# Graph attention layer and routed experts: first stage with fewer sort steps, skip projection moved, running maxima raised in place

## The chip, the cores and the metric

One core of one Trainium2 chip runs the whole kernel. The metric is the device time of one execution in microseconds (us). The engines are PE (matrix products), DVE (vector), ACT (scalar functions), POOL (GpSimd, which here issues the gathers) and SP (which issues most other DMAs).

## The reference

The input has 6250 nodes with 256 features, and 200000 edges sorted by their destination. First comes a layer norm and one attention layer on the graph, then a small attention that routes nodes to four experts, on 131072 other edges, which are not sorted.

```python
def _gnn_layer(x, edge_index, Wq, bq, Wk, bk, Wv, bv, Wskip, bskip, gamma, beta):
    q = (x @ Wq + bq).reshape(n, HEADS, D)          # 8 heads of 32
    k = (x @ Wk + bk).reshape(n, HEADS, D)
    v = (x @ Wv + bv).reshape(n, HEADS, D)
    logits = einsum('ehd,ehd->eh', q[dst], k[src]) / sqrt(D)
    seg_max = segment_max(logits, dst)
    expv = exp(logits - seg_max[dst])
    attn = expv / segment_sum(expv, dst)[dst]
    agg = segment_sum(attn[:, :, None] * v[src], dst)
    out = agg.reshape(n, HID) + (x @ Wskip + bskip)
    y = x + gelu(out)
    return (y - mean(y)) / sqrt(var(y) + 1e-05) * gamma + beta
# then: h = x @ W_gat, attention over the routing edges, layer norm, mean over heads,
# the best two of four experts, softmax of their scores, and the experts' FFN
...
out = out + g[..., None] * (gelu(x @ W1[ei] + b1[ei]) @ W2[ei] + b2[ei])
```

## The kernel before

**Stages.** The kernel runs five stages, one after the other: `prepare`, `attend` (the walk over the edges), `node_update`, `route_experts` and `route_gates`. Inside a stage each engine has its own order of instructions, written out by hand, and counters (semaphores) tie them together. The change touches the first three stages.

**prepare.** Nodes lie in 49 tiles of 128. For each tile ACT normalises x with moments that DVE made for three parts of x (`X_PARTS`), PE turns the tile (`turn`, L474) and multiplies it with four weights at once: key and value in one bank, query and skip in another (L498 is the bias, L500 the two halves of the product). ACT evacuates. The query is kept as three bf16 numbers that sum to it: ACT rounds the high part, POOL subtracts it (L271), ACT rounds the middle part, POOL subtracts that (L275). At the same time DVE sorts the 131072 routing edges by a bitonic network of 17 levels: pairs of instructions (L307, L308) compare and merge 512 columns each, and where partners lie on different partitions PE flips the array through its transposes (L514) and DVE and ACT copy it back (L354, L611). There are `FLIPS` = 15 flips; `BETWEEN` gives how many tiles PE and ACT do ahead of each. After the last flip DVE takes sources and destinations from the keys (L438 to L442), and a few products make tables of which window and group each later step uses (L444 to L462). SP stores the tiles.

**attend.** A step handles four tiles of 128 edges; there are 439. POOL gathers the 128 rows of key and value that a tile of edges needs (L746, a ring of eight groups). PE picks the queries with one-hot matrices (L966), DVE multiplies and sums to logits (L847, L851), and maxima per node and per step are made with a scan (L803) and PE. The running maximum of the nodes in a window of 128 is kept negated in `m_all`. In a step DVE makes the new maximum (L816), the message of the step before (L839, value times weight), scales the window's sums in PSUM (L834), makes the fall of the maximum (L821), works on later steps, and keeps the new maximum (L825). ACT makes the factor exp(fall) (L936) and the weights (L920). PE's `differences` (L984, L986) waits for the new maximum and for the message that frees its bank:

```python
def differences(s):
    pe.wait_ge(ok["m_new"], s.v + 1)
    if there(s + (-1)):
        pe.wait_ge(ok["msg"], s.v)
```

PE then adds the messages to the window's sums (L1013), and ACT copies these out (L897). Every instruction that depends on a step's window reads its number into a register first.

**node_update.** Seven blocks of seven tiles. DVE divides the sums by the denominators (L1171, L1173, L1176), adds the skip projection (L1181), ACT applies gelu (L1217), DVE adds x (L1192) and makes two layer norms with ACT's square roots (L1221, L1225), POOL adds beta to the kept x (L1260), PE turns the result and makes the routing products h (L1272, L1279). A block's load is x normalised, skip and x, 2688 KB.

## Time and profile before

| | |
|---|---|
| median of 3 runs | 5862.63 us (5853.13 to 5880.14) |
| the profiled execution | 5876.38 us, span 5874.6 us |
| busy over the span | PE 67%, DVE 59%, POOL 44%, ACT 43% |
| granted TensorE clock, mean | 0.806 of full speed |
| gathers of the edge walk (L746) | 1564, 1482.7 us busy |
| gathers of the routing (L1389) | 1024, 974.5 us busy |

An engine's busy share is an average over stages with different limits; what a stage costs is seen in the stretch of the trace that belongs to it, and a wait there is put down to what came last.

### The profile page before, as it was taken

The page shows a single profiled execution, that of the slowest core. Times are in us where ns is not written, and L with a number is a line of the kernel's source. Part 1 is how long each engine was busy: PE and PEld are TensorE (multiplying, and loading weights), DVE is VectorE, ACT ScalarE, POOL GpSimd, SP SyncE. Part 2 cuts the span into 40 slices and gives each one's busy share as a digit, 9 for nine tenths or more (in the row PEclk, how much of TensorE's full clock was granted, in tenths as well). Part 3 has the DMA queues.
Part 4 walks back from the last instruction along what each step waited for, and adds up shares of the span by engine and source line. Part 5 has one row for each costly group of instructions (what it writes and reads, how often), then busy time and mean ns, then how long its engine had stood idle before and what let it go on. Part 6 is the DMA issues. An engine that isn't in the chain of part 4 may idle for free. (4 is left out here: it accounts for less than half of the span.)

```text
span 5874.6 us, 106076 instructions
## 1 busy us (share of the span) xinstructions
PE 3912.2 (67%) x26108; PEld 2753.9 (47%) x26109; DVE 3464.7 (59%) x9273; ACT 2543.2 (43%) x6305; POOL 2589.4 (44%) x2723
## 2 busy tenths in 40 slices
PE   7857777777777777777777773355666666666550
PEld 3335555555555556555555563233434343443330
DVE  8856666666666666666666668434444444444348
ACT  4445555555555555554555555223333333333320
POOL 3244444444444444444445441444444444445540
PEclk9978888888888888888888885577877787777765
DMA  6455555555555555555556555111111111111117
GB/s 212 147 163 165 155 168 163 163 161 168 156 159 163 161 168 156 165 158 165 154 166 172 159 150 177 44 15 18 21 19 21 19 21 19 22 18 19 20 21 263
DMA packets 367690, 683.50 MB, mean 116 GB/s; under 512 B 70294, under 2 KB 240482, under 8 KB 367074
## 3 DMA queue, kind: packets, MB, share of 16 engines
q0 software_dynamic: 157888, 427.05, 27.9%
q1 hardware_dynamic: 183106, 223.68, 11.5%
q10 hardware_dynamic: 26080, 25.70, 1.5%
q8 instruction: 246, 4.03, 0.3%
q14 instruction: 370, 3.03, 0.2%
HBM read 588.41 MB, written 87.78 MB: 115 GB/s over the span
## 5 line engine op out<-in xcount | busy, mean ns | idle before, releaser
L746 POOL DMA_INDIRECT KV<-kv_d,src_i x1564 | 1482.7, 948 | 1677.7 <-DVE msg L839 1232.4
L1389 POOL DMA_INDIRECT re_src<-src_tab_d,rsrc x1024 | 974.5, 952 | 978.7 <-SPq L1399 675.7
L1013 PE MATMUL agg_ps<-msg,oh 128*128 128x264 f32 x3512 | 1085.8, 455 | 229.7 <-issue 218.4
L1013 PEld LDWEIGHTS agg_ps<-msg,oh 128*128 128x128 f32 x3512 | 744.4, 222 | 414.2 <-issue 282.7
L1597 PE MATMUL ex_y_ps<-ex_w,ex_hid 128*112 128x256 f32 x1792 | 586.6, 461 | 301.6 <-issue 299.1
L966 PE MATMUL Q<-q,ohT 128*128 128x256 bf16 x5328 | 753.0, 297 | 15.6 <-issue 13.9
L839 DVE TENSOR_TENSOR msg<-KV,weigh_ps 128x1056 f32<-128x1056 f32 x439 | 545.7, 1243 | 268.6 <-ACT weigh_ps L920 250.1
L1516 ACT COPY re_ohT<-re_ohT_ps 128x1024 bf16<-128x1024 bf16 x179 | 181.0, 1011 | 1075.0 <-remote 1010.6
L966 PEld LDWEIGHTS Q<-q,ohT 128*128 128x128 bf16 x5328 | 531.4, 105 | 117.4 <-issue 19.5
L909 ACT ACTIVATE square<-iota_b,off 128x128 bf16<-128x128 bf16 x1784 | 569.2, 392 | 0.3
L1597 PEld LDWEIGHTS ex_y_ps<-ex_w,ex_hid 128*112 128x112 f32 x1792 | 363.7, 214 | 434.1 <-issue 366.0
L847 DVE TENSOR_TENSOR prod<-KV,Q 128x1024 f32<-128x1024 f32 x443 | 536.1, 1210 | 46.3 <-remote 29.0
L851 DVE TENSOR_REDUCE lg<-prod 128x32 f32<-128x1024 f32 x443 | 540.5, 1220 | 15.1
L897 ACT COPY acc<-agg_ps 128x264 f32 x439 | 166.8, 380 | 701.5 <-remote 400.5
L1585 PE MATMUL ex_h<-acc,ex_w 128*128 (+1 forms) x896 | 446.0, 623 | 20.3 <-issue 16.3
L834 DVE TENSOR_TENSOR agg_ps<-agg_ps,fac 128x264 f32<-128x264 f32 x439 | 190.1, 433 | 405.2 <-issue 263.1
L1466 DVE TENSOR_TENSOR ex_y<-ex_y_ps,ex_b 112x256 f32<-112x256 f32 x224 | 89.9, 418 | 543.3 <-PE ex_y_ps L1597 344.6
L920 ACT ACTIVATE weigh_ps<-weigh_ps 128x32 f32<-128x32 f32 x439 | 80.0, 182 | 648.8 <-remote 560.7
L956 PE MATMUL ohT_ps<-ident_b,oh 128*128 128x128 bf16 x1784 | 208.1, 236 | 198.8 <-issue 170.7
L912 ACT ACTIVATE oh<-square,one 128x512 bf16<-128x512 bf16 x446 | 321.9, 722 | 14.5
L916 ACT COPY ohT<-ohT_ps 128x512 bf16<-128x512 bf16 x445 | 252.3, 567 | 162.5 <-remote 143.2
L807 DVE TENSOR_REDUCE tile_max<-turned_ps 128x8 f32<-128x32 f32 x439 | 83.7, 191 | 380.0 <-remote 377.3
(264 smaller groups left out, 6199.0 us busy)
## 6 DMA issues: line engine op xcount, KB each, us to landing
q<-q_d SPq DMA_DIRECT2D x446, 192.0 KB
y_d<-ex_y ACTq DMA_DIRECT2D x56, 448.0 KB
rg_ye<-y_d SPq DMA_DIRECT2D x7, 3584.0 KB, 11.8
KV<-kv_d,src_i POOLq DMA_INDIRECT x1564
nu_xs<-xs_d SPq DMA_DIRECT2D x7, 2688.0 KB, 11.9
re_src<-src_tab_d,rsrc POOLq DMA_INDIRECT x1024
kv_d<-pr_kv SPq DMA_DIRECT2D x49, 260.0 KB, 2.2
xs_d<-pr_xs SPq DMA_DIRECT2D x49, 256.0 KB, 2.4
```

Source lines behind the costliest of these rows:

```text
L746: pool.indirect_dma_start(out=KV[:, t % (KVR * G), :], out_offset=None, in_=k.kv_d, in_offset=bass.IndirectOffsetOnAxis(ap=k.src_i[:, t:t ...
L839: v.tensor_tensor(m[:, :, :, :], KV[:, tiles(s), D:KVW].rearrange("p t (h e) -> p t h e", e=HW), bc(p_ps.rearrange("p (t h) -> p t h", h=H ...
L847: v.tensor_tensor(prod[:, :, :], KV[:, tiles(s), 0:D], Q[ring(s, 2)][:, :, :], ALU.mult).then_inc(ok["prod"], 1)
L851: v.reduce_sum(lg[s.slot][:, :], prod[:, :, :].rearrange("p t (h d) -> p (t h) d", d=DH), AX.X).then_inc(ok["lg"], 1)
L909: q = act.activation(square[:, t, :], k.iota_b[:, :], ACT.Square, bias=off[s.slot][:, t:t + 1])
L912: act.activation(oh[ring(s, OHR)][:, :, :], square[:, :, :], ACT.Relu, bias=k.one[:, :], scale=-1.0).then_inc(ok["oh"], 1)
L916: act.copy(ohT[ring(s, OHR)][:, :, :], ohT_ps[:, :, :]).then_inc(ok["ohT"], 1)
L966: m = pe.matmul(Q[ring(s, 2)][:, t, :], ohT[ring(s, OHR)][:, t, :], q3[s.slot][:, c * D:(c + 1) * D], start=(c == 0), stop=(c == 2))
L1013: m = pe.matmul(agg_ps[:, 0:HEADS * HW], oh32[ring(s, 2)][:, t, :], msg[ring(s, 2)][:, t, :, :].rearrange("p h e -> p (h e)"), start=False ...
L1389: pool.indirect_dma_start(out=gs[:, t % (RING * RG), :], out_offset=None, in_=k.src_tab_d, in_offset=bass.IndirectOffsetOnAxis(ap=k.rsrc[: ...
L1585: m = pe.matmul(h_ps[f % 2][:, 0:UN], k.w1_sb[:, u.at % NE, c, f * P:(f + 1) * P], k.xT[:, bass.ds(u.block, 1), c, half * UN:(half + 1) * ...
L1597: m = pe.matmul(y_ps[w % 2][0:YN, 0:D], hid[u.at % 2][:, f, w * YN:(w + 1) * YN], k.w2_sb[:, u.at % NE, f, :], start=(f == 0), stop=(f == ...
```

## The change

In `prepare` the skip projection leaves the tile loop, and with it its quarter of the weights. The turned, normalised tile (`xt`) is stored to memory in its place. POOL's two subtractions for the query are replaced by PE adding the rounded part times minus the identity in the query's bank; ACT now rounds all three parts from there. DVE starts the sort after the moments of the first part (now ten tiles), and makes the other moments within levels 3 and 6. The last level of the sort stops before its last two flips: the order that is left within a group of eight columns isn't sorted out, outputs are rearranged by group, and a group's largest destination comes from a reduction with a transpose and a product. `FLIPS` is 13, and five tiles come after the last flip.

In `attend` the maxima are kept in bf16. DVE makes the rise before the message and raises the maximum in place after it; ACT makes the fall from the rise with a Relu, and then the factor. PE's differences read the maxima themselves, so PE reads the window's number too.

In `node_update` PE makes the skip projection from the turned tiles, two blocks ahead, and ACT copies it to where the sums will be added. DVE's seven multiplications per block become one in place and one addition.

```diff
 class prepare
-        X_PARTS = ((0, 7), (7, 28), (28, NW))
-        FLIPS = 15
+        X_PARTS = ((0, 10), (10, 28), (28, NW))
+        FLIPS = 13
-        BETWEEN = (20, 2, 2, 2, 2, 2, 2, 2, 2, 2, 2, 2, 2, 2, 3)
+        BETWEEN = (20, 2, 2, 2, 2, 2, 2, 2, 2, 2, 2, 2, 2)
...
+                    sp.wait_ge(ok["xt"], w + 1)
+                    sp.dma_start(k.xt_d[w, :, :], xt[w % LOOP][:, :, :].rearrange("p c n -> p (c n)")).then_inc(xs_stored[w % LOOP], 16)
+                    sp.dma_start(k.xs_d[rows, 0:D], xs[w % LOOP][:, :]).then_inc(xs_stored[w % LOOP], 16)
...
-                        pool.tensor_tensor(resid[w % 2][:, :], qf[w % 2][:, :], q3[w % PS][:, 0:D], ALU.subtract).then_inc(ok["resid"], 1)
...
-                        pool.tensor_tensor(q3[u % PS][:, 2 * D:3 * D], resid[u % 2][:, :], q3[u % PS][:, D:2 * D], ALU.subtract).then_inc(ok["lo"], 1)
...
-                moments(1)
-                moments(2)
...
                 for level in range(1, 10):
-                    if level in (4, 5):
-                        scales(level - 3)
+                    if level in (3, 6):
+                        moments(level // 3)
+                    if level in (5, 8):
+                        scales(level // 3)
...
-                    for b in (9, 8, 7):
-                        plain(P << (b - 7))
-                    flip(meanwhile.get(held["flips"], lambda: None))
-                    for b in range(6, -1, -1):
-                        plain(1 << b)
-                flip()
+                    if level < 17:
+                        for b in (9, 8, 7):
+                            plain(P << (b - 7))
+                        flip(meanwhile.get(held["flips"], lambda: None))
+                        for b in range(6, -1, -1):
+                            plain(1 << b)
...
+                d.on(v.tensor_reduce(group_max[:, :], by_group(k.rdst[:, :]), AX.X, ALU.max))
                 ready.append((d.n, 0))
-                d.on(v.tensor_scalar(k.rsrc[:, :], bits, SRC_MASK, None, ALU.bitwise_and))
+                d.on(v.tensor_scalar(by_group(k.rsrc[:, :]), bits, SRC_MASK, None, ALU.bitwise_and))
                 v.wait_ge(ok["tab_products"], 4)
+                d.on(v.tensor_reduce(most[:, :], tab_ps[:, 3 * P:4 * P], AX.X, ALU.max))
+                wait()
+                d.on(v.tensor_scalar(most_diag[:, :], k.ident[:, :], most[:, 0:1], None, ALU.mult))
...
+                def less_hi(w):
+                    pe.wait_ge(ok["rounded"], HIGH(w))
+                    pe.matmul(q_ps[w % 2], minus[:, :], q3[w % PS][:, 0:D], start=False, stop=True,
+                              skip_group_check=True).then_inc(ok["less"], 1)
...
-                    for bank, at in ((kv_ps[p], 0), (qs_ps[p], 2 * D)):
-                        pe.matmul(bank[:, :], ones3[:, :], b_parts[:, at:at + 2 * D], start=True, stop=False)
-                        for c in range(2):
-                            m = pe.matmul(bank[:, :], xt[p][:, c, :], w_sb[:, c, at:at + 2 * D], start=False, stop=(c == 1))
-                    m.then_inc(ok["products"], 1)
+                    project(kv_ps[p][:, :], 0, 2 * D, w, (lambda: less_hi(w - 1)) if w else (lambda: None)).then_inc(ok["kv_made"], 1)
+                    if w:
+                        less_mid(w - 1)
+                    if w >= 2:
+                        pe.wait_ge(ok["rounded"], LOW(w - 2))
+                    project(q_ps[p], 2 * D, D, w).then_inc(ok["products"], 1)
...
+                    if w in (5, 12):
+                        root(w // 5)
...
-                    if w in (1, 3):
-                        root((w + 1) // 2)

 attend
+                def rise(s):
                     v.wait_ge(ok["tile_max"], s.v + 1)
                     if there(s + (-1)):
                         v.wait_ge(ok["m_all"], s.v)
-                    v.scalar_tensor_tensor(out=m_new[ring(s, 2)][:, :], in0=tile_max[:, :], scalar=-1.0, in1=node_max(s),
-                                           op0=ALU.mult, op1=ALU.min).then_inc(ok["m_new"], 1)
...
-                    v.tensor_tensor(m_fall[ring(s, 2)][:, :], m_new[ring(s, 2)][:, :], node_max(s), ALU.subtract).then_inc(ok["m_fall"], 1)
...
-                    v.tensor_scalar(node_max(s), m_new[ring(s, 2)][:, :], 1.0, None, ALU.mult).then_inc(ok["m_all"], 1)
+                    v.scalar_tensor_tensor(out=m_rise[ring(s, 2)][:, :], in0=tile_max[:, :], scalar=-1.0, in1=node_max(s),
+                                           op0=ALU.mult, op1=ALU.subtract).then_inc(ok["m_rise"], 1)
+
+                def raise_max(s):
+                    v.wait_ge(ok["m_rise"], s.v + 1)
+                    if there(s + (-1)):
+                        v.wait_ge(ok["dl"], s.v)
+                    v.scalar_tensor_tensor(out=node_max(s), in0=tile_max[:, :], scalar=-1.0, in1=node_max(s),
+                                           op0=ALU.mult, op1=ALU.min).then_inc(ok["m_all"], 1)
...
                     if there(s):
+                        rise(s)
+                    if there(s + (-1)):
+                        message(s + (-1))
+                    if there(s):
                         raise_max(s)
                     if there(s + (-1)):
-                        message(s + (-1))
                         scale_sums(s + (-1))
-                    if there(s):
-                        fall(s)
...
-                    if there(s):
-                        keep_max(s)
...
+                        act.wait_ge(ok["m_rise"], s.v + 1)
+                        act.activation(m_fall[:, :], m_rise[ring(s, 2)][:, :], ACT.Relu, scale=-1.0).then_inc(ok["m_fall"], 1)
                         act.wait_ge(ok["m_fall"], s.v + 1)
-                        act.activation(fac[ring(s, 2)][:, :], m_fall[ring(s, 2)][:, :], ACT.Exp, scale=SCALE).then_inc(ok["fac"], 1)
+                        act.activation(fac[ring(s, 2)][:, :], m_fall[:, :], ACT.Exp, scale=-SCALE).then_inc(ok["fac"], 1)

 node_update
+                    if not last:
+                        sp.wait_ge(s_skip, i * PAIRS + PAIRS)
+                        load_turned(i + 2, s)
...
-                    for w in range(CW):
-                        ch.on(v.tensor_tensor(v4(out[s][:, :, :])[:, w], k.acc[:, bass.ds(i * CW + w, 1), :].rearrange("p a (h e) -> p (a h) e", e=HW)[:, :, 0:DH],
-                                              bc(den[:, w, :, :], [P, HEADS, DH]), ALU.mult))
+                    flat = k.acc[:, bass.ds(i * CW, CW), :].rearrange("p w (h e) -> p (w h) e", e=HW)[:, :, 0:DH]
+                    ch.on(v.tensor_tensor(flat, flat, bc(den[:, :, :, :].rearrange("p w h a -> p (w h) a"), [P, CW * HEADS, DH]), ALU.mult))
                     ch.wait()
                     ch.done()
-                    v.wait_ge(landed[s], j * 16 + 16)
-                    v.tensor_tensor(out[s][:, :, :], out[s][:, :, :], xs[s][:, :, D:2 * D], ALU.add).then_inc(s_in, 1)
+                    v.wait_ge(s_kept, (i + 1) * PAIRS)
...
+                def keep_skip(i, s, cs):
+                    if i >= 2:
+                        act.wait_ge(norm, i - 1)
+                    for c in cs:
+                        n = min(2, CW - 2 * c)
+                        act.wait_ge(s_skip, i * PAIRS + c + 1)
+                        act.copy(out[s][:, 2 * c:2 * c + n, :], skip_ps[c % 2][:, 0:n, :]).then_inc(s_kept, 1)
...
+                    if i + 2 < NB:
+                        keep_skip(i + 2, s, (0, 1))
                     root(1, i * 2 + 2)
...
+                project(0)
+                project(1)
                 for i in range(NB):
+                    if i + 2 < NB:
+                        project(i + 2)
                     turn(i // 2, i % 2, i < 2, i == NB - 1)
```

## Rows read from the trace of the kernel before

**Rows 1.** Windows, four stages: PE, PEld, DVE, ACT, POOL busy, granted clock, DMA share, GB/s.

```profile
0.00:339.30 339.30, 270.81 (x759) 114.57 (x760) 289.08 (x497) 148.91 (x458) 100.52 (x126) 0.94 0.50 174
339.30:3543.70 3204.40, 2376.38 (x18103) 1830.75 (x18103) 2076.55 (x4402) 1662.61 (x4879) 1482.74 (x1564) 0.85 0.56 161
3543.70:3733.80 190.10, 64.05 (x294) 60.46 (x295) 146.86 (x334) 95.75 (x161) 31.11 (x8) 0.53 0.49 165
3733.80:5700.00 1966.20, 1189.40 (x6800) 738.71 (x6800) 816.13 (x3663) 624.61 (x789) 975.06 (x1026) 0.77 0.13 19
```

**Rows 2.** One line of the first stage: ns min/median/max, first and last start.

```profile
L307 DVE TENSOR_TENSOR so_key<-so_key x136: 691/693/1194, 47.5 to 323.8; 128x512 f32<-128x512 f32 x136
```

**Rows 3.** Groups of the first stage: busy us, mean ns | idle before.

```profile
L275 POOL TENSOR_TENSOR pr_q<-pr_resid,pr_q 128x256 bf16<-128x256 f32 x49 | 51.7, 1056 | 0.0
...
L308 DVE TENSOR_TENSOR so_key<-so_key 128x512 f32<-128x512 f32 x136 | 108.6, 799 | 0.0
```

**Rows 4.** Timeline of a step of the walk (start us, us, engine, line, operation).

```profile
2023.30 0.16 DVE L825 TENSOR_SCALAR m_all<-m_new 128x8 bf16 x1
...
2023.37 0.18 DVE L807 TENSOR_REDUCE tile_max<-turned_ps 128x8 f32<-128x32 f32 x1
...
2023.95 1.24 DVE L839 TENSOR_TENSOR msg<-KV,weigh_ps 128x1056 f32<-128x1056 f32 x1
...
2026.28 0.25 PE L986 MATMUL weigh_ps<-m_new,ohT 128*128 128x8 bf16 x4
...
2026.99 0.18 ACT L920 ACTIVATE weigh_ps<-weigh_ps 128x32 f32<-128x32 f32 x1 [0.18 <-issue]
...
2028.60 1.24 DVE L839 TENSOR_TENSOR msg<-KV,weigh_ps 128x1056 f32<-128x1056 f32 x1
```

**Rows 5.** Busy time in a stretch early in the walk.

```profile
367.00:384.80 17.80, 0.09 (x1) 0.00 (x0) 0.00 (x0) 0.00 (x0) 9.74 (x11) 0.50 0.66 191
```

**Rows 6.** DVE's waits in the walk: us in total, times, longest us.

```profile
DVE tile_max L807 <- remote: 377.3, 98, 5.6
...
DVE msg L839 <- ACT weigh_ps L920: 250.1, 135, 6.2
```

**Rows 7.** Timeline of ACT in the first block of the node update.

```profile
3560.24 1.70 ACT L1217 ACTIVATE nu_out<-nu_out 128x1792 f32<-128x1792 f32 x1
```

**Rows 8.** Timeline of a block of the node update.

```profile
3611.35 6.21 DVE L1176 TENSOR_TENSOR nu_out<-acc,nu_den 128x256 f32<-128x256 f32 x7
3612.95 3.99 POOL L1260 TENSOR_TENSOR nu_xs<-nu_xs,nu_bet 128x1792 f32<-128x1792 f32 x1 [18.88 <-DMA nu_xs<-xs_d]
...
3615.80 6.17 PE L1279 MATMUL nu_h<-nu_wg,acc 128*128 128x24 f32 x28 [4.61 <-ACT acc L1232]
...
3626.90 0.30 ACT L1221 ACTIVATE nu_rstd<-nu_mv,nu_eps 128x7 f32<-128x7 f32 x1 [4.14 <-DVE nu_mv L1158]
```

**Rows 9.** Timeline of DVE in the opening.

```profile
14.05 0.20 DVE L293 RECIPROCAL pr_rstd<-pr_rstd 128x7 f32<-128x7 f32 x1 [4.98 <-ACT pr_rstd L536]
...
29.51 6.95 DVE L283 BATCH_NORM_STATS2 pr_stats<-acc 128x6 f32<-128x256 f32 x21 [4.32 <-DMA acc<-in_x_dram]
...
37.91 0.66 DVE L393 TENSOR_SCALAR so_ends<-so_ends 128x1024 int32<-128x1024 int32 x1
```

**Rows 10.** Timeline of PE, the products of a tile's first bank.

```profile
26.33 3.78 PE L500 MATMUL pr_kv_ps<-pr_w,pr_xt 128*128 128x512 f32 x4
...
42.63 1.98 PE L500 MATMUL pr_kv_ps<-pr_w,pr_xt 128*128 128x512 f32 x4
...
47.31 1.98 PE L500 MATMUL pr_kv_ps<-pr_w,pr_xt 128*128 128x512 f32 x4
```

**Rows 11.** Timeline of DVE in the last level of the sort.

```profile
295.35 0.69 DVE L354 COPY so_key<-so_flip 128x512 f32<-128x512 f32 x1 [0.75 <-PE so_flip L514]
...
310.78 0.69 DVE L308 TENSOR_TENSOR so_key<-so_key 128x512 f32<-128x512 f32 x1
...
331.45 0.70 DVE L438 TENSOR_SCALAR so_dst_i<-so_key 128x1024 int32<-128x1024 int32 x1 [0.47 <-ACT so_key L611]
```

More of the change, by code:

```diff
@@ L170, in prepare @@
                  "w_in", "b_in", "b_rounded", "b_rest", "b_ready", "stats", "norm", "sqrt",
-                 "xn", "turned", "xt", "products", "kv", "skip", "qf", "hi", "resid", "mid", "lo")
+                 "xn", "turned", "xt", "products", "kv_made", "kv", "rounded", "less")
         ok = {n: nc.alloc_semaphore(f"pp_{n}") for n in names}
@@ L195, in order @@
                 flip(f)
-            assert w == NW
+            while w < NW:
+                tile(w)
+                w += 1
         with nc.Block() as block:
@@ L523, in _ @@
                 order(tile, flip)
+                less_hi(NW - 1)
+                less_mid(NW - 1)
                 pe.wait_ge(ok["table"], table_at["lasts"])
                 pe.wait_ge(ok["sort"], ready[FLIPS][0])
-                pe.matmul(tab_ps[:, 0:RNG], ends[:, :], k.rdst[:, RG - 1:RT:RG], start=True, stop=True).then_inc(ok["tab_products"], 1)
+                pe.transpose(tab_ps[:, 3 * P:4 * P], group_max[:, :], k.ident[:, :]).then_inc(ok["tab_products"], 1)
                 pe.wait_ge(ok["sort"], ready[FLIPS + 1][0])
+                pe.matmul(tab_ps[:, 0:RNG], ones[:, :], most_diag[:, :], start=True, stop=True).then_inc(ok["tab_products"], 1)
+                pe.wait_ge(ok["sort"], ready[FLIPS + 2][0])
                 pe.matmul(tab_ps[:, 0:RNS], ones[:, :], r_passed[:, :], start=True, stop=True).then_inc(ok["tab_products"], 1)
@@ L566, in evacuate @@
                              kv_ps[p][:, D:2 * D].rearrange("p (h d) -> p h d", d=DH)).then_inc(ok["kv"], 1)
-                    act.copy(xs[w % LOOP][:, D:2 * D], qs_ps[p][:, D:2 * D]).then_inc(ok["skip"], 1)
+                    if w:
+                        low(w - 1)
+                    high(w)
                 def rows(b):
@@ L699, in attend @@
         agg_ps = ps("agg_ps", [P, 512], F32)
-        names = ("tiles", "used", "off", "square", "oh", "turned", "ohT", "q", "prod", "lg", "running", "scans",
-                 "seg_max", "maxima", "tile_max", "m_new", "m_fall", "m_all", "fac", "dl", "p", "msg", "oh32", "agg",
-                 "scaled", "acc", "cleared", "emptied", "resets_seen")
+        names = ("tiles", "off", "square", "oh", "turned", "ohT", "q", "prod", "lg", "running", "scans",
+                 "seg_max", "maxima", "tile_max", "m_rise", "m_fall", "m_all", "fac", "dl", "p", "msg", "oh32", "agg",
+                 "scaled", "acc", "cleared")
         ok = {n: nc.alloc_semaphore(f"at_{n}") for n in names}
@@ L980, in differences @@
                 def differences(s):
[L981 removed]
+                    w = window(s)
+                    pe.wait_ge(ok["m_all"], s.v + 1)
                     if there(s + (-1)):
@@ L995, in group, with window, enter @@
                     return groups[s.offset]
+                def window(s):
+                    if s.offset not in windows:
+                        windows[s.offset] = load(pe, k.w_tab, s, NW - 1)
+                    return windows[s.offset]
+                def enter():
+                    groups.clear()
+                    windows.clear()
                 def maxima(s):
@@ L1073, in node_update @@
         TC = RD + 2 * RH
-        xs = [sb(f"nu_xs{i}", [P, CW, 3 * D], F32) for i in range(2)]
+        xs = [sb(f"nu_xs{i}", [P, CW, 2 * D], F32) for i in range(2)]
+        xt = [sb(f"nu_xt{i}", [P, CW, 2 * P], F32) for i in range(2)]
+        ws = sb("nu_ws", [P, 2, D], F32)
         den = sb("nu_den", [P, CW, HEADS, 1], F32)
@@ L1249, in turn @@
                     normalise(1, x2[s], xn2).then_inc(xn_ok, 1)
+                    if i + 2 < NB:
+                        keep_skip(i + 2, s, range(2, PAIRS))
+                for i in range(2):
+                    keep_skip(i, i, range(PAIRS))
                 gelu(0, 0)
-                pairs(act, half, turn)
+                for i in range(NB):
+                    turn(i // 2, i % 2, i < 2, i == NB - 1)
                 copies(NB - 1)
@@ L1264, in _, with project @@
                 pe.wait_ge(ready, 5)
+                def project(i):
+                    s = i % 2
+                    pe.wait_ge(xt_landed[s], (i // 2 + 1) * 16)
+                    for c in range(PAIRS):
+                        n = i * PAIRS + c
+                        if n >= 2:
+                            pe.wait_ge(s_kept, n - 1)
+                        pair = range(2 * c, min(2 * c + 2, CW))
+                        pe.matmul(skip_ps[c % 2][:, 0:len(pair), :], k.ones3[:, :], k.skip_bias[:, 0:len(pair), :], start=True, stop=False)
+                        for w in pair:
+                            for f in range(2):
+                                m = pe.matmul(skip_ps[c % 2][:, w % 2, :], xt[s][:, w, f * P:(f + 1) * P], ws[:, f, :],
+                                              start=False, stop=(w == pair[-1] and f == 1))
+                        m.then_inc(s_skip, 1)
                 def turn(j, s, first, last):
```

205 lines of the change are left out of this document (113 added, 92 removed).

## Prediction

> **What bounds the kernel now.** I read the busy time by stage first, then in each changed stage the timeline of the engine with the least idle time, and the waits and grouped lines for sizes. The profiled execution took 5876.4 us round a span of 5874.6; the median of the runs is 5862.6, which is 13.8 less. The sum is made against the profile, and 13.8 then taken off.
>
> Preparing takes 339.3 us, the walk over the edges 3204.4, the node update 190.1, routing and experts 1966.2 [rows 1], the gates what is left. The last two stages keep their instructions but for one semaphore that both rings of gathers now share; I count them at nothing, with 3 us either way. What the change is worth lies in the first three.
>
> In the first stage DVE is busy 289 of 339 us [rows 1]. Its work is the sort: 136 pairs of compare and merge (L307, L308). One of 512 columns takes 0.69 us, but up to 1.19 [rows 2], and L308's mean is 0.80 [rows 3]. The long ones are those beside which POOL subtracts q's remainders (L275 and L271, 49 each, 1.06 us for L275 [rows 3]). L308's excess is 136 × (0.799 − 0.69) = 15 us; with L307's 12 and what the copies, reductions and moments of the stage suffer in the same way I get 38, of which some 32 after level 6 has begun.
>
> The Trainium skill (SBUF — State Buffer, on the port pair of VectorE and GpSimd) says that a VectorE instruction with two SBUF inputs and a GpSimd one shut each other out for a whole instruction. The trace agrees: 1.19 us where the median is 0.69.
>
> In the walk a step in which nothing is late takes 4.65 us, and DVE runs back to back in it: message at 2023.95, the next at 2028.60 [rows 4]. The mean over 439 steps is 7.2 us (3204.4 [rows 1] less the ends, over 439). The rest is stalls. Early in the stage 17.8 us hold one PE instruction and 11 gathers of POOL [rows 5]; the same in small shows as DVE's 377 us of waiting for the first maximum, 98 times, and 250 us for ACT's weights, 135 times [rows 6]. A DVE instruction saved counts only where a step is DVE's.
>
> In the node update seven blocks of seven tiles take 190.1 us, of which 16.5 pass before the first gelu at 3560.24 [rows 7]: 24.8 a block. In its middle DVE has the work of [rows 8] and its like, with hardly a gap.
>
> **The change, part by part.**
>
> First stage, opening. DVE now finishes all moments before the sort: the first part's scales are asked for at 14.05, the sort's set-up begins at 37.9 [rows 9]. With the moments of parts 1 and 2 moved into levels 3 and 6 it begins some 23.5 us earlier. But the moments themselves stay, 39 tiles at 0.33 (6.95 for 21 [rows 9]) with their totals, 14 us, and three tiles more in part 0, 1.4 with their wait. And ACT's square root for part 1 is issued in its tile 5. PE's tiles begin at 26.3, the first at half speed, and follow each other at 4.68 us (42.63 to 47.31) [rows 10], so ACT is there near 49.6, and DVE waits some 10 us for it at level 5. With the first 6 us of contention gone too, level 6 begins 23.5 − 14 − 1.4 + 6 − 10 = 4 us sooner: **−4**.
>
> First stage, contention. POOL's 98 subtractions go; PE does them as products of bf16 with minus the identity, ACT rounds out of PSUM. That gives back **−32** if the sort stays what ends the stage. PE's tile gets shorter: four float32 products of 512 columns are 1.98 us, twice a tile [rows 10]; the half with q and skip shrinks to q alone, −0.93 and −0.16 for its bias, and two small products cost 2 × 0.11 (a quarter of a float32 one of twice the width): about 3.85 for 4.68. ACT trades two copies and a cast for three copies, and the two copies of the skip half go.
>
> First stage, end. The last level stops before its last two flips. From DVE's copy of the flip before (295.35) to the pair that ends at 310.78 + 0.69 = 311.5 all is as now; gone is what lies between that and the first output at 331.45: two flips with their waits and seven pairs, **−20.0** [rows 11]. Added are the group maxima, one reduction over 1024 columns (1.2, by the message's 1.24 for 1056 [rows 4]), a transpose, a reduction, a diagonal and a product: two trips to PE, each about the 0.75 us that a flip's copy waits [rows 11], and two small instructions. The outputs are now written with a stride: 0 to 3. **+5** in all. And 5 tiles (49 less 20 and 12 × 2) come after the last flip. That flip's copy falls near 259 (295.4 less 4 and 32), and five tiles of 3.85 with the remainders end at 280 to 282 at full clock; the table's last products stand behind them on PE. DVE is at the table near 284, so PE just fits; at the speed of the first tile, 3.78 for 1.98 [rows 10], it would end at 290 to 298. The sum is −51; I take **−50**, bounds −58 and −40.
>
> Walk. DVE's three small instructions for the maximum (new, fall, keep) become two (rise, raise in place). A small one's price from start to start is 0.07 us (2023.30 to 2023.37), while it is listed at 0.16 [rows 4]. So 0.07 × 439 = 31, upper bound 0.16 × 439 = 70. As 60% of the steps are DVE's own (the others carry the waits of [rows 6]), **−18**. Against it: PE's differences (L986) now wait for a maximum raised after the message, where they waited for one made before it. But they wait for that message already (it frees their bank), and in a clean step they start at 2026.28, 1.1 us after it has ended at 2025.19 [rows 4]; raising takes 0.07 of that. ACT gets a Relu and a wait of its own before the factor's exponential, 0.2 to 0.3, ahead of the weights. These start at 2026.99 and the message that needs them at 2028.60 [rows 4], so it fits; but where DVE already waits for them, 135 times [rows 6], each wait can grow by 0.1 to 0.2, 13 to 27 us. PE also loads the window's register in each step, in the time in which it now waits for DVE's `running`. Bounds −60 and +30.
>
> Node update. Of a block's 2688 KB 1792 stay, and 896 of turned x come: the same bytes. DVE's seven multiplications become one, 6.21 us now [rows 8]. But in the 6.21 one instruction waits out POOL's addition of beta (3612.95, 3.99 [rows 8]), and that addition stays: the seven alone would be some 2.8, the merged one 2, so the gain is 0.4 to 1.5 us a block. If the two engines did not shut each other out, it would be 4, and the sum 18 us lower over the stage; the rule of the Trainium skill named above speaks against that. New is PE's projection, 28 float32 products of 256 columns and 4 bias products a block, two blocks ahead. By 0.25 us a product warm and 0.47 at half speed (halves of [rows 10]), the 16 before ACT's first two copies take 4.4 or 8.6 us with their bias. They stand behind PE's h, which ends at 3615.80 + 6.17 [rows 8]. So ACT's copies end at 3627.1 to 3631.3 (with 0.7 for the copy), and ACT's order has them ahead of the square root that is now at 3626.90 [rows 8]: each of five blocks gets 0.2 to 4.4 later where DVE would allow 1.5 sooner. I take 1 later for each, +5. At the start gelu(0), now at 3560.24 [rows 7], waits for 56 products and 8 biases, 14 us warm and 26 cold, from about 3552.5 on, and for ACT's eight copies: +13. The last two blocks have no projection ahead: −3. **+15**, bounds −3 and +35.
>
> Sum: −50 − 18 + 15 = −53. Profile 5823, median 5862.6 − 53 = **5810 us**.
>
> **Rivals.** A measurement of this kernel can tell 0.5%, 29 us, from no change.
>
> A, the sum above: 5810, its own range 5785 to 5832. Chance 0.55.
>
> B, the walk gives the whole listed time: −70 in place of −18. For it: a clean step has no gap on DVE. Against: the 377 us in which DVE waits [rows 6] while POOL gathers are no instruction's. −50 − 70 + 15 = −105, 5758. Chance 0.17.
>
> C, the walk gives nothing, since the weights come later by what DVE saves, and the projection runs at half speed: −50 + 0 + 35 = −15, 5848, within 0.5%. For it: PE's granted clock in the node update is 0.53 of full [rows 1], near the lower of its two levels (1.2 GHz), and 28 products of 24 columns take 6.17 us there. Against: the projection itself fills PE. Chance 0.22.
>
> D, the other side: ACT's Relu with its wait isn't hidden. If its 0.3 us come on top in each of 439 steps, that is +132, less DVE's 31: −50 + 101 + 15 = +66, 5929. It decides from +64 net in the walk (0.15 us a step): from there the kernel is slower by over 0.5%. Against it: the 1.4 us between weights and message in a clean step. Chance 0.06.
>
> **How the numbers follow.** The likeliest is A, 5810. The range, 5762 to 5856, reaches nearly to B's time and over C's; out of it are D and the far half of B, some 0.16. Faster by over 0.5% (under 5833) are A, B and a part of C: 0.76. Same is the rest of C: 0.18. Slower 0.06.
>
> **What would show it.** In the changed profile: the sort's pairs all near 0.69; DVE at level 5 waiting some 10 us for ACT's square root; the stage's end near 289; a clean step at 4.58; DVE's wait for the weights between 250 and 280 us; the merged multiplication near 6 beside POOL's addition; gelu(0) some 29 us after the stage's start; later blocks no more than 1 us longer. The prediction is wrong if DVE's waits in the walk grow by over 80 us or the walk shortens by over 60: the walk's is the term with the widest bounds. It is also wrong if PE's last five tiles, not the sort, end the first stage.

## The result, and the profile after

The changed kernel takes 5994.5 us (median of 4, 5969.1 to 6008.1) against 5870.5 for the one before (4 runs): a ratio of 1.020, with a 95% interval of 1.017 to 1.023. The forecast was 5810, with 5762 to 5856 as its range. The change made the kernel slower; whether by more or by less than 2% these runs leave open.

The stages of the profiled execution, in the columns of [rows 1]:

```profile
0.00:294.10 294.10, 230.01 (x842) 116.95 (x843) 240.96 (x476) 141.72 (x408) 8.65 (x28) 0.95 0.59 200
294.10:3628.20 3334.10, 2424.41 (x18103) 1862.23 (x18103) 2049.10 (x3964) 1796.37 (x5318) 1482.80 (x1564) 0.84 0.54 155
3628.20:3850.00 221.80, 130.76 (x518) 102.46 (x519) 137.75 (x292) 109.57 (x189) 30.33 (x7) 0.68 0.46 142
3850.00:5871.90 2021.90, 1190.87 (x6952) 746.61 (x6952) 842.07 (x3789) 632.25 (x802) 973.88 (x1026) 0.76 0.12 19
```

Beside [rows 1] the first stage is 45 us shorter, the node update 32 longer, and the walk 3334 for 3204, some 130 longer. (From the first instruction of the routing to the first of the gates the fourth stage is 2021.9 for 2006.2; the window in [rows 1] ends a little earlier.) DVE has less to do in the walk than it had, 2049 for 2077 us; what grew is its waiting. These are its longest waits there (us, times, longest), to be read beside [rows 6] and, first, the two rows of the scaling of the sums in the kernel before, where it is L834:

```profile
DVE agg_ps L834 <- issue: 263.1, 85, 6.7
...
DVE agg_ps L834 <- ACT acc L897: 141.9, 95, 8.1
```

```profile
DVE agg_ps L867 <- issue: 321.1, 79, 7.8
DVE agg_ps L867 <- ACT acc L929: 293.0, 91, 8.2
DVE tile_max L841 <- remote: 280.0, 75, 5.2
DVE msg L872 <- ACT weigh_ps L952: 271.7, 209, 6.6
```

The wait for the first maximum fell by 97 us. The one before the scaling of the sums (L867) rose, from 142 to 293 us where ACT's copy of the sums (L929) released it, and from 263 to 321 where nothing shown did. All of DVE's waits in the walk together grew from 1108 to 1264 us. I call a *freeze* a stretch in which DVE and ACT start nothing and PE hardly anything while POOL gathers on. One step with a freeze, in the timelines of POOL, DVE and ACT:

```profile
2018.17 0.95 POOL L780 DMA_INDIRECT KV<-kv_d,src_i  x1 [0.30 <-issue]
...
2023.18 0.95 POOL L780 DMA_INDIRECT KV<-kv_d,src_i  x1 [0.30 <-issue]
```

```profile
2016.92 1.24 DVE L872 TENSOR_TENSOR msg<-KV,weigh_ps 128x1056 f32<-128x1056 f32 x1
2018.09 0.15 DVE L857 SCALAR_TENSOR_TENSOR m_all<-tile_max,m_all 128x8 f32 x1
2026.39 0.44 DVE L867 TENSOR_TENSOR agg_ps<-agg_ps,fac 128x264 f32<-128x264 f32 x1 [8.16 <-ACT acc L929]
```

```profile
2016.49 0.18 ACT L952 ACTIVATE weigh_ps<-weigh_ps 128x32 f32<-128x32 f32 x1 [0.33 <-PE weigh_ps L1021]
2025.91 0.38 ACT L929 COPY acc<-agg_ps 128x264 f32 x1 [9.24 <-remote]
2030.21 0.18 ACT L952 ACTIVATE weigh_ps<-weigh_ps 128x32 f32<-128x32 f32 x1 [0.33 <-issue]
```

The two gathers shown are the fourth and the last of eight in a row, a *burst*; the first starts at 2014.41. POOL gathers on while ACT and DVE stand still from 2019 to 2025.8. ACT's copy didn't get in before the freeze. After it ACT has to go through the copy and its whole turn of 4.3 us to the weights, and only then DVE can make a message. I looked at all bursts of eight gathers without a pause in the two timelines (127 before, 125 after) and took times from the start of the burst's first gather. Before, ACT's copy started within 5.2 us in 72 of 127, after in 46 of 125. Where it did, the message behind the freeze came at 12.2 to 12.3 us in both kernels; where it didn't, at 13.5 before and 14.8 after. The mean is 12.83 before and 13.84 after, and 1.01 us × 125 = 126 us, about the walk's loss of 130. This says where in the walk the time went, not yet why.

### The profile page after: what moved, and what is told of

It reads as the page before. It is cut to its first block and busy times, and to the rows that moved or that the text cites. A ratio compares the mean times of both kernels' runs of the same rounds, so it can differ in the third digit from the quotient of the medians.

```text
span 6006.2 us, 109049 instructions
## 1 busy us (share of the span) xinstructions
PE 3976.1 (66%) x26415; PEld 2828.3 (47%) x26416; DVE 3379.6 (56%) x8773; ACT 2683.5 (45%) x6722; POOL 2495.7 (42%) x2625
## 5 line engine op out<-in xcount | busy, mean ns | idle before, releaser
L1058 PE MATMUL agg_ps<-msg,oh 128*128 128x264 f32 x3512 | 1103.2, 463 | 128.5 <-issue 87.1
L929 ACT COPY acc<-agg_ps 128x264 f32 x439 | 166.5, 379 | 860.0 <-remote 606.4
L867 DVE TENSOR_TENSOR agg_ps<-agg_ps,fac 128x264 f32<-128x264 f32 x439 | 190.8, 435 | 614.2 <-issue 321.1
L990 PE MATMUL ohT_ps<-ident_b,oh 128*128 128x128 bf16 x1784 | 210.5, 237 | 184.9 <-issue 144.0
L1021 PE MATMUL weigh_ps<-m_all,ohT 128*128 x1756 | 138.2, 168 | 254.8 <-issue 254.6
L1670 PE MATMUL re_agg<-re_split,re_oh 128*128 128x60 bf16 x1408 | 81.4, 201 | 318.3 <-issue 212.5
## 6 DMA issues: line engine op xcount, KB each, us to landing
rg_ye<-y_d SPq DMA_DIRECT2D x7, 3584.0 KB, 12.2
nu_xs<-xs_d SPq DMA_DIRECT2D x7, 1792.0 KB, 10.3
```

Of the source, the lines that this page charges most:

```text
L990: m = pe.transpose(ohT_ps[:, t, :], oh[ring(s, OHR)][:, t, :], k.ident_b[:, :])
L1058: m = pe.matmul(agg_ps[:, 0:HEADS * HW], oh32[ring(s, 2)][:, t, :], msg[ring(s, 2)][:, t, :, :].rearrange("p h e -> p (h e)"), start=False ...
```

## The experiments

Chips differ more than the kernels do. The profiles before the prediction and the result above come from chips with freezes, and so do relu_early, weights_sooner, copies_late and tiles_spread, all four on one chip, on which the kernel before took 5986 us. All other runs fell on chips on which the kernel before takes 4070 to 4074 us. There its walk takes 2085 us (in old_walk, since the kernel before has no profile there), and I find no stretch of over 2 us in which PE starts products or weight loads only every 0.6 to 1.7 us, against 112 to 157 in the profiles of the other kind, except for 9 in weights_sooner. First stage, node update and gates take the same time on both within 5 us. Each ratio below is to the kernel before on the same chip; where an expectation gives a walk of 3200 us and more, it was written for a chip with freezes.

**The walk alone, and everything but the walk.** old_walk is the changed kernel with the function `attend` of before, new_walk_only the kernel before with the changed one:

```diff
 old_walk:       the changed kernel
-    attend of the changed kernel, m_all in bf16
+    attend of before, m_all in f32
 new_walk_only:  the kernel before
-    attend of before, m_all in f32
+    attend of the changed kernel, m_all in bf16
```

> The changed kernel with the edge walk of before (float32 maxima, fall and keep on DVE, one exponential for the factor on ACT). In the profiles the walk went from 3205 to 3334 us. Both theories of what lengthened it expect the walk back at 3205 within 15 us; the first stage stays at 294 and the node update at 219 to 222, so that the whole comes to 0 to 20 us beside the kernel before. If the walk stays near 3330, the cause lies in what the first stage leaves behind (the clock, the tables, the order of rows in memory) and not in the walk's own code.

> The kernel before with the edge walk of the changed kernel alone. Both theories expect the walk at 3320 to 3345 us and the whole 115 to 140 us over before. If the walk's loss comes from something else of the change, the whole is within 0.3% of before.

old_walk: 0.9954 (0.9938 to 0.9971), walk 2085.0, first stage 293.4, node update 221.0. new_walk_only: 1.0305 (1.0288 to 1.0323), walk 2206.7. So the loss is in the walk's own code, 122 us (2206.7 less 2085.0), without a single freeze.

**The two suspects, each added to the kernel before.**

```diff
 relu_added
+                        act.activation(spare[:, :], m_fall[ring(s, 2)][:, :], ACT.Relu, scale=-1.0).then_inc(ok["spare"], 1)
+                        act.wait_ge(ok["spare"], s.v + 1)
                         act.activation(fac[ring(s, 2)][:, :], m_fall[ring(s, 2)][:, :], ACT.Exp, scale=SCALE).then_inc(ok["fac"], 1)
 window_loaded
                     if there(s) and not last:
                         group(s + 2)
+                        window(s + 1)      # PE: load(pe, k.w_tab, s, NW - 1)
```

> The kernel before, with one thing more: ahead of ACT's exponential for the factor stands a Relu of the fall into a spare buffer that nothing reads, and the exponential waits for it. Theory ACT: the wait on its own result empties ACT's queue, its two register loads are no longer hidden, so the weights come about 0.7 us and the copy of the sums about 0.4 us later in each step; the freeze that follows 5 us after a burst of gathers begins then catches the copy before it has gone through. It expects most of the loss here: walk 3300 to 3340. Theory PE (differences wait for the maximum raised in place, and PE loads one register more): walk within 20 us of 3205.

> The kernel before, with one thing more: PE loads the window's register in each step, as in the changed kernel (nothing uses it). Theory ACT: walk within 25 us of 3205, as the load lies in PE's wait for the running maxima. Theory PE: walk longer by 60 us or more, since PE's first product of a step comes 0.5 us later.

relu_added: 1.0035 (1.0022 to 1.0048), walk 2101.5. window_loaded: 1.0188 (1.0171 to 1.0205), walk 2161.2. Theory ACT, on which I had put the loss, expected both wrongly here: on this chip the Relu is worth 15 to 17 us and PE's register load 76. Together that is 92 of the 122, although DVE has less to do in the changed walk, so the two cost more together than each alone. But the sub-step of theory ACT is seen: in relu_added's clean steps (those under 4.9 us) ACT's weights start 4.17 us after DVE's message, in old_walk's 3.38, for an instruction of 0.19 and its wait. Where ACT loads its registers, before `off` and before the weights, the gaps open. From `off` to the weights it is 0.20 us in old_walk and 0.63 in relu_added:

```profile
1501.22 0.30 ACT L935 ACTIVATE off<-dst_f,wbase 128x4 f32 x1
1501.41 0.18 ACT L954 ACTIVATE weigh_ps<-weigh_ps 128x32 f32<-128x32 f32 x1
```

```profile
1504.86 0.30 ACT L902 ACTIVATE off<-dst_f,wbase 128x4 f32 x1
1505.49 0.18 ACT L921 ACTIVATE weigh_ps<-weigh_ps 128x32 f32<-128x32 f32 x1 [0.33 <-issue]
```

By the medians 0.43 of the 0.79 us lie there, 0.14 ahead of `off`, and 0.22 are the Relu's.

**The two suspects, each moved within the changed kernel.** In relu_early and weights_sooner the Relu's result is asked for long after it is there; weights_sooner also makes the weights earlier:

```diff
 relu_early
+                        act.activation(m_fall[ring(s, 2)][:, :], m_rise[ring(s, 2)][:, :], ACT.Relu, scale=-1.0)...
                     if there(s + 7):
                         one_hot(s + 7)
                     if there(s):
-                        act.activation(m_fall[:, :], m_rise[ring(s, 2)][:, :], ACT.Relu, scale=-1.0)...
                         act.wait_ge(ok["m_fall"], s.v + 1)
 weights_sooner, relu_early and:
-                    if there(s + (-1)):
-                        weights(s + (-1))
...
                         act.activation(fac[ring(s, 2)][:, :], ..., ACT.Exp, scale=-SCALE)...
+                        weights(s)
```

> The changed kernel; ACT's Relu stands ahead of the one-hot instructions instead of right before the exponential that waits for it (and m_fall has two buffers). The number of instructions is the same. Theory ACT (the wait on its own result is what costs): the walk comes back from 3334 to 3200 to 3240. If the Relu costs by its own time, and not by the wait, or if PE is the cause, it stays at 3320 to 3335.

> As relu_early, and ACT makes the weights of a step right behind the step's factor, ahead of the one-hot copy and the register loads, instead of at the head of its next turn. Theory ACT: the weights are then ready 1 us sooner than in the kernel before and more of the steps get through before a freeze: walk 3120 to 3200. If ACT's order isn't what the freeze catches, no different from relu_early within 20 us.

Both ran where there are freezes. relu_early: 0.996 (0.9945 to 0.9975), walk 3281.3. Two kernels with the changed walk untouched ran on the same chip, copies_late and tiles_spread (below), with 3410.0 and 3429.4 us, so the place of the Relu is worth 129 to 148 us there. The 3200 to 3240 that theory ACT expected weren't reached; on this chip the changed walk takes 76 to 95 us longer than in the result. In 71 of its 119 bursts of eight ACT's copy got in within 5.2 us, in the two others in 42 of 133 and 48 of 135. weights_sooner: 1.0415 (1.0397 to 1.0432), walk 3531.3, a miss by over 300 us. Nearly every step there is 8.2 us (351 of 438 between 8 and 9), and POOL gathers in bursts of four, one for each step, where the others mostly have eight for every second one: the walk fell into another rhythm, with 9 stretches of slow PE where relu_early has 116. So what a shift in ACT's order brings on such a chip isn't given by how much sooner an instruction is.

**PE's register load moved to where products are queued.** Where window_loaded had shown the cost, this takes it away:

```diff
 window_inside: PE
-                def sums(s):
+                def sums(s, between=lambda: None):
...
                     for t in range(G):
+                        if t == 2:
+                            between()          # window(s + 1)
                         m = pe.matmul(agg_ps[:, 0:HEADS * HW], oh32[ring(s, 2)][:, t, :], ...
...
                     if there(s) and not last:
                         group(s + 2)
-                        window(s + 1)
 both_moved: window_inside and relu_early
```

> The changed kernel itself, on the chip on which the next three run. Chips differ: on one the walk of before takes 2085 us and shows no freeze at all, on the others 3205 and more with some 110 to 160 of them. Expected where there is no freeze: 1.022 to 1.030 of before (walk +118 by new_walk_only, the rest -18 by old_walk); where there are freezes: 1.015 to 1.024.

> The changed kernel; PE loads the window's register between the second and the third tile of the sums, where eight products are queued, and not behind its group's load at the end of the turn. Theory PE (the load makes PE's order longer than DVE's): on a chip without freezes the mean step goes from 4.95 to 4.65 to 4.75 us, the walk from 2207 to 2080 to 2110 and the whole to 0.5 to 2% under the kernel before less what the node update costs; with freezes 40 to 100 us less than the changed kernel. Theory ACT alone: within 20 us of the changed kernel.

> window_inside_2, and ACT's Relu ahead of the one-hot instructions as in relu_early. If the two costs are separate, then without freezes 0 to 12 us less than window_inside_2 (the Relu with its wait cost 12 in relu_added), with freezes a walk no longer than that of the kernel before; if there was one cause only, no difference from the better one of the two.

changed_2: 1.0289 (1.0272 to 1.0306), walk 2216.0. window_inside_2: 0.9949 (0.9933 to 0.9966), walk 2089.5. both_moved_2: 0.9869 (0.9853 to 0.9886), walk 2053.3. The last is 36 us under window_inside_2 where 0 to 12 were expected: with PE's load out of the way the Relu's place is worth more than in relu_added. PE's differences still wait for the maximum raised behind the message, so that cost, not tested alone, doesn't show. The profile shows what the load did, in PE's wait ahead of its first product of a step (L1009), first in changed_2, then in window_inside_2:

```profile
PE turned_ps L1009 <- issue: 183.6, 294, 1.2
```

```profile
PE turned_ps L1009 <- DVE running L837: 54.6, 135, 4.3
...
PE turned_ps L1009 <- issue: 2.1, 10, 0.3
```

A step of changed_2 in PE's timeline:

```profile
1503.63 2.03 PE L1058 MATMUL agg_ps<-msg,oh 128*128 128x264 f32 x8
1505.49 0.39 PE L990 MATMUL ohT_ps<-ident_b,oh 128*128 128x128 bf16 x4
1506.73 0.27 PE L1009 MATMUL turned_ps<-ident,lg 128*32 128x128 f32 x1 [0.85 <-issue]
```

Two loads stand behind the last product, and nothing is queued over them. PE's next step begins 1.24 us after L990. With PE late like this, DVE's message at 1505.95 waited 0.60 for the weights. What one load costs there: from the start of the four transposes to the next step's first product it is 1.14 us in window_loaded (median of the 213 steps with no other wait) and 0.56 in old_walk, so nearly 0.6. The mean step is 4.98 us in changed_2, 4.69 in window_inside_2 and 4.60 in both_moved_2; its median in the last is 4.53.

**Once more, meant for a chip with freezes.** These too fell on chips without.

> window_inside again. On a chip with freezes: if PE's load costs there what it does without them, the walk is 100 to 130 us shorter than that of changed_3; if the phase of the step against the bursts decides, less than 40 or the other way. On the chip without: 0.993 to 0.997 of before, as measured.

> both_moved again. On a chip with freezes: if both moves hold, the walk is below that of before by up to 30 us (DVE's 0.08 us a step) and the whole at 0.985 to 0.995; if the phase decides, anywhere from 0.98 to 1.04. On the chip without: 0.985 to 0.989, as measured.

> The changed kernel on the chip of the other runs of this call, for their stages. With freezes 1.015 to 1.030 of before, without 1.027 to 1.031.

> window_inside again. On a chip with freezes: if PE's load costs there what it does without them, the whole is at 0.995 to 1.005 of before; if the phase of the steps against the bursts decides, 1.01 to 1.04. On a chip without: 0.993 to 0.997, as measured.

They repeat the numbers, all within what was expected for such a chip: window_inside_3 0.9958 (0.9941 to 0.9974), window_inside_4 0.9961 (0.9946 to 0.9976), both_moved_3 0.9857 (0.9841 to 0.9874), changed_3 1.0273 (1.0252 to 1.0294).

**Node update: copies behind the second root.** late_copies_2 has it with the walk of before.

```diff
 copies_late: ACT, turn
-                    if i + 2 < NB:
-                        keep_skip(i + 2, s, (0, 1))
                     root(1, i * 2 + 2)
                     act.wait_ge(back, (i + 1) * KB)
                     normalise(1, x2[s], xn2).then_inc(xn_ok, 1)
                     if i + 2 < NB:
-                        keep_skip(i + 2, s, range(2, PAIRS))
+                        keep_skip(i + 2, s, range(PAIRS))
```

> The changed kernel; in the node update ACT makes all four copies of the skip projection after the second normalisation, none ahead of the second square root. The square root waited in the profile until 3703.82 though its variance was ready at 3699.2: 2 copies that wait for PE at half clock, and a table load of 1.28 behind them. Theory: 4.0 us less for each of five blocks, node update 219 to 222 becomes 200 to 205. Rival (PE's projection delays PE's transposes and h, whoever waits ahead): within 5 us of 219, since PE now stands still behind its third pair until the copies come.

> The changed kernel with the walk of before and ACT's copies of the skip projection after the second normalisation. By the stages measured so far: first stage 294 for 339, walk as before, node update 205 for 190, which is 25 to 35 us under the kernel before on either kind of chip. If the change in the first stages reaches the walk through what it leaves behind, the walk differs from that of before by more than 15 us.

copies_late: 1.0231 (1.0209 to 1.0253), node update 205.4 for 221.8, walk 3410.0. late_copies_2: 0.9909 (0.9892 to 0.9925), node update 206.6, walk 2086.8, first stage 291.9; the whole is 39 us under the kernel before, 4 more than the most that was expected. The 16 us came as expected; in copies_late they are lost in a walk that is 76 us longer than that of the result, on another chip. In the changed kernel's profile this is the place (ACT):

```profile
3699.44 0.59 ACT L1285 COPY nu_out<-nu_skip_ps 128x512 f32<-128x512 f32 x1 [5.69 <-PE nu_skip_ps L1352]
...
3701.92 0.59 ACT L1285 COPY nu_out<-nu_skip_ps 128x512 f32<-128x512 f32 x1 [1.90 <-PE nu_skip_ps L1352]
...
3702.52 1.28 ACT L1289 ACT_TABLE_LOAD   x1
3703.82 0.30 ACT L1289 ACTIVATE nu_rstd<-nu_mv,nu_eps 128x7 f32<-128x7 f32 x1
```

DVE's variance was ready at 3699.16. The root came 4.7 us later: PE's first pair at the low clock (its eight products take 3.78 us at a granted clock of 0.50, those of the second pair 2.07 at 0.96), the second pair, and the square root's table, which in the kernel before was loaded right behind the gelu, in ACT's idle time. In the three blocks after that one the late root cost something more. DVE's small instruction behind it, 0.17 us where POOL does nothing, met POOL's addition and took 3.27, 3.13 and 2.49 us; this is the first:

```profile
3731.56 3.96 POOL L1335 TENSOR_TENSOR nu_xs<-nu_xs,nu_bet 128x1792 f32<-128x1792 f32 x1 [19.78 <-DMA nu_xs<-xs_d]
```

```profile
3732.27 3.27 DVE L1223 SCALAR_TENSOR_TENSOR nu_shift<-nu_mv,nu_rstd 128x7 f32<-128x7 f32 x1
```

**First stage: the five last tiles spread.**

```diff
-        BETWEEN = (20, 2, 2, 2, 2, 2, 2, 2, 2, 2, 2, 2, 2)
+        BETWEEN = (20, 3, 3, 3, 3, 3, 2, 2, 2, 2, 2, 2, 2)
```

> The changed kernel; the five node tiles that come after the last flip of the sort are put between earlier flips (one more ahead of flips 2 to 6). DVE waited 7.1 us for PE's last tiles at the end of the first stage. Theory: 5 to 7 us less, the first stage ends at 287 to 289. Rival: PE is then late at the flips themselves, three tiles take longer than the levels between two flips there, and DVE waits there what it saved at the end: 293 to 300.

tiles_spread: 1.0268 (1.025 to 1.0286), first stage 298.7 for 294.1. The rival holds: DVE's waits for flips are 27.0 us there, 13.7 in the changed kernel, and the 7.1 at the end are gone.

**Everything together**, both_moved with copies_late:

> both_moved with ACT's copies of the skip projection after the second normalisation. 14 to 18 us under both_moved_3 on either kind of chip (node update 221 to 205), if nothing in the stages behind it moves.

> all_mended again. On a chip with freezes: 0.975 to 0.99 of before if both moves hold there; if the phase decides, anywhere from 0.97 to 1.04. On a chip without: 0.981 to 0.985, as measured.

all_mended: 0.9827 (0.981 to 0.9843), all_mended_4: 0.9823 (0.9805 to 0.984); walk 2052.1, node update 205.0 in the first. The whole is 13 us under both_moved_3 where 14 to 18 were expected. On chips without freezes this is the fastest kernel here, 71 us under the one before. Where there are freezes it was not run.

## Why the prediction was wrong

**First stage, −45 for −50: near, but partly by errors that cancel.** Every such instruction of the sort now takes 0.69 us, as this row shows for L310, which was L307 [rows 2]:

```profile
L310 DVE TENSOR_TENSOR so_key<-so_key x126: 691/692/695, 27.5 to 275.3; 128x512 f32<-128x512 f32 x126
```

With POOL's subtractions gone not one of 126 is long. That agrees with the Trainium skill (SBUF — State Buffer, "Who interferes with whom"), by which a VectorE instruction with two SBUF inputs and a GpSimd one that reads SBUF hold each other up for a whole instruction. DVE waited 7.7 us for ACT's square root at level 5, where I had said 10. But the opening gave 1.6 us and not 4 (level 6 begins at 70.3, before at 71.9), and from there to the last flip's copy the sort gained 27.5 and not 32, so that copy came at 266.3 and not 259. Behind it the sum was wrong the other way. It kept the 16.1 us that lie between 295.35 and 311.5 in the kernel before [rows 11], but the change also drops the three pairs of bits 9, 8 and 7 from the last level (4.0 us, in the diff as `if level < 17`), and no instruction is long any more: it took 10.3. DVE was ready at 281.1 and not 284. The five tiles and their remainders ended on PE at 287.8, and DVE waited for the table's product behind them:

```profile
288.16 0.29 DVE L448 TENSOR_REDUCE so_most<-pp_tab 128x1 f32<-128x128 f32 x1 [7.11 <-PE pp_tab L552]
```

So PE's tiles ended the stage, which the prediction named as what would make it wrong; the wait is 7.1 us.

**Walk, +130 for −18: the step that failed.** The gain on DVE was there: the median step went from 4.61 us in old_walk to 4.53 in both_moved_2, the 0.07 to 0.08 from start to start and not the listed 0.16, and both_moved_2 has it in full, 2053.3 for 2085.0. What failed is the cost put beside it at nothing. The prediction had PE's second register load "in the time in which it now waits for DVE's `running`", and gave it no term in the sum. The profile of before had the row against it:

```profile
PE turned_ps L975 <- DVE running L803: 68.9, 100, 3.4
```

PE has that wait in 100 of 439 steps. Where there are no freezes it is 54.6 us in 135 steps with the load away (window_inside_2), 0.4 in each, and a load is nearly 0.6. Shown: with PE's load moved among queued products the walk is 127 us shorter there.

The prediction also said that the Relu costs 0.2 to 0.3 us and fits. It moves the start of the weights by 0.8 (relu_added), as ACT's register loads, hidden before, come out from under its instructions; that is 15 to 36 us without freezes. With freezes the Relu's place is worth 129 to 148, by relu_early. There the whole is at 0.996 of before with PE's load still in its place. Less the other stages that leaves 5310 us for walk and routing, against 5321 before (an estimate, with the stages of the profile of before, as that kernel has none on this chip). So on the kind of chip of the prediction moving the Relu alone takes the loss back. The result there isn't the sum of both costs. The burst times above suggest the reason, that the place of ACT's copy against the burst decides how a step gets through; weights_sooner shows that an earlier instruction can also turn out worse. The prediction's own sign of being wrong, waits of DVE that grow by over 80 us, came true with 156.

Rival D had the right side, and for chips with freezes the right instruction, with 101 us net from ACT's Relu not being hidden. It was given 0.06, and its 5929 is still 65 under the result. Its way (0.3 us in each of 439 steps) isn't what happened: a clean step of the changed kernel takes 4.55 us for 4.65, and the loss is one us per burst of gathers. That no term or rival had PE's load is the larger gap, since without freezes it is the larger cost.

**Node update, +32 for +15: a term mis-sized.** gelu(0) starts 29.1 us after the stage does (3657.3 less 3628.2), as forecast. The blocks are the miss. From gelu(0) to the second root of the first block it is 19.7 us (3657.32 to 3677.01), before 20.6; from one second root to the next 26.8, 27.9, 30.2, 30.4, 21.5 and 18.3, before 22.7, 23.3, 23.9, 23.7, 23.6 and 17.9. So the five blocks with a projection ahead are 4.2 later on average, where the sum had 1, and three of them, with 4.6, 6.3 and 6.7, lie outside the prediction's bounds of 0.2 to 4.4. The last two together gave 1.7 and not 3. The low clock for the first pair, at 3.78 us for eight products, was in the upper bound. A table load of 1.28 us behind the copies wasn't, nor were the 2.3 to 3.1 us that DVE's small instruction takes longer in three blocks, beside POOL's addition, now that the root is late. copies_late takes the copies out of the root's way, and the same distances are 23.7 to 24.3. DVE held up by POOL is there as said, but in one block it fell on the new addition (5.67 us for 2.02), and never on the merged multiplication.

**Routing, 16 us more for none.** Its code doesn't differ but for one semaphore. Without freezes it takes 1311 to 1316 us with and without the change (1320 in new_walk_only). On the one chip with freezes the same routing code took 2024 to 2056 in four kernels, so that 16 us are within what that stage varies by there. Why it varies wasn't tested.

What stays open: how much PE's load costs on a chip with freezes (relu_early had it in its walk and was level with before), why the two costs are more than their sum without freezes, and what makes a freeze, or spares some chips.

## What to carry to other kernels

Count a register load as an instruction of the engine's order: give it a place with products queued over it, and don't put two behind the last one. A wait of an engine on its own last result can cost more than the result's time (here 0.8 us for 0.22), since what was hidden behind queued work comes out; put other work between. And when two engines are nearly full, as PE (1996.6 us) and DVE (1993.6) in the 2053.3 us of both_moved_2's walk, count on an instruction saved on one only after the other is shown to have room for what it gets.

## What the runs showed of the hardware

Two kinds of chip run the kernel before at 4070 and at 5860 to 5990 us. For the changed kernel the granted clock is nearly the same on both in the first stage (0.94 and 0.95) but 0.99 and 0.84 over the walk. In the step shown the slower kind stands nearly still from 5 us into a burst of back-to-back gathers (1.25 us apart) to 2.7 us past the start of its last one; in 6.5 us of this freeze, 2019.3 to 2025.8 of the changed kernel, DVE and ACT started nothing:

```profile
2019.30:2025.80 6.50, 2.33 (x24) 1.71 (x25) 0.00 (x0) 0.00 (x0) 3.80 (x4) 0.87 0.78 226
```

A burst alone doesn't make a freeze: on the other kind the gathers come at the same pace, old_walk has 45 bursts of 16 and more, and none of them has one.

On the slower kind the Relu's place moved the walk by 129 to 148 us down (relu_early), and the weights' place put it 250 above that (weights_sooner). On the other the Relu's place moved it by 36, and the place of PE's register load by 127. A result from one kind of chip doesn't carry to the other without its own run.
